# Octonion feed-forward kernel: weights loaded in 16-partition pieces from two queues, and the first ternary set ahead of x's rounding

## What is computed

```python
def ternary_dequant(W):
    scale = jnp.mean(jnp.abs(W))
    return scale * jnp.clip(jnp.round(W / scale), -1.0, 1.0)
...
gate = oct_ternary_linear(xp, w_gate)      # w_gate: 8 x 341 x 128, float32
up   = oct_ternary_linear(xp, w_up)        # w_up:   8 x 341 x 128
h    = silu(gate) * up
out  = oct_ternary_linear(hp, w_down)      # w_down: 8 x 128 x 341
```

## Time and profile before

| | |
|---|---|
| median of 3 runs | 593.52 us (593.51 to 593.63) |
| profiled execution: its own time | 593.39 us |
| profiled execution: its span | 591.4 us |
| TensorE matmul busy | 579.9 us, 98% of the span |
| VectorE, ScalarE, GpSimd busy | 510.1, 356.9, 457.3 us |
| DMA | 30.67 MB, mean 52 GB/s |

### The profile page before, as it was taken

How to read it: one execution, slowest core, us unless ns; L and a number is a source line. 1 busy time by engine, 2 the same in 40 slices (tenths; PEclk the granted TensorE clock), 3 DMA queues, 4 the chain that set the end, 5 groups by cost and what they waited for, 6 DMA issues and landing times.

```text
span 591.4 us, 16418 instructions
## 1 busy us (share of the span) xinstructions
PE 579.9 (98%) x6750; PEld 539.9 (91%) x6750; DVE 510.1 (86%) x1230; ACT 356.9 (60%) x497; POOL 457.3 (77%) x362
## 2 busy tenths in 40 slices
PE   7999999999999999999999999999999999999996
PEld 7999998899989998999989998999989998998996
DVE  4987978889997999979997999979997999958854
ACT  5788995654586456664586456664586555543540
POOL 3417569998699977998699977998699977997920
PEclk9999999999999999999999999999999999999999
DMA  9720220002210112002210212002210202002021
GB/s 208 166 73 1 72 73 2 2 2 73 108 38 1 73 54 92 3 1 73 103 42 1 74 46 99 2 2 73 97 47 2 72 3 72 2 3 72 2 73 73
DMA packets 10251, 30.67 MB, mean 52 GB/s; under 512 B 928, under 2 KB 4032, under 8 KB 10176
## 3 DMA queue, kind: packets, MB, share of 16 engines
q1 hardware_dynamic: 10176, 29.62, 15.9%
HBM read 21.23 MB, written 8.39 MB: 50 GB/s over the span
## 4 chain that ended last, share of the span: by engine, by line
POOL 50%; issue 28%; PE 7%; ACT 1%; DVE 1%; POOLq 0%; ACTq 0%
POOL hop L1382 15%; POOL hs L1376 9%; POOL hs L1372 9%; POOL hs L1377 9%; PE acc L496 5%; POOL hs L1371 5%; PE acc L391 1%; POOL r L1330 1%; ACT pk L638 0%; ACT pk L624 0%; POOL hop L1379 0%; PE acc L384 0%; ACT wd L703 0%; POOL onep L1341 0%; POOL vr L1328 0%
## 5 line engine op out<-in xcount | busy, mean ns | idle before, releaser
L496 PE MATMUL acc<-wd,hop 114*128 114x128 f16 (+1 forms) x2944 | 170.7, 219 | 0.7 <-POOL hop L1382 0.7
L496 PEld LDWEIGHTS acc<-wd,hop 114*128 114x128 f16 (+1 forms) x2944 | 167.4, 98 | 1.9 <-POOL hop L1382 0.9
L722 ACT ACTIVATE pk<-acc 114x512 f32<-114x512 f32 (+1 forms) x120 | 70.7, 590 | 83.6 <-PE acc L384 49.5
L1371 POOL TENSOR_TENSOR hs<-hx 114x512 f32<-114x512 f32 x47 | 59.8, 1273 | 55.5 <-DVE hx L1127 52.1
L1382 POOL TENSOR_TENSOR hop<-hs,hop 114x1024 f16<-114x1024 f32 x46 | 98.2, 2135 | 2.7 <-ACT hop L777 2.7
L1379 POOL TENSOR_TENSOR hop<-hx,hop 114x1024 f16<-114x1024 f32 x46 | 98.3, 2137 | 1.3 <-ACT hop L766 1.3
L384 PE MATMUL acc<-xop,wu 128*128 128x256 f16 x704 | 84.2, 273 | 1.0 <-DVE hx L1127 0.7
L1030 DVE TENSOR_TENSOR bd<-acc,pk 114x256 f32<-114x256 f32 (+1 forms) x104 | 43.5, 418 | 48.2 <-ACT pk L722 48.2
L384 PE MATMUL acc<-xop,wg 128*128 128x256 f16 x704 | 84.2, 273 | 0.1
L391 PE MATMUL acc<-xop,wu 128*128 128x256 f16 x704 | 84.1, 273 | 0.1
L391 PE MATMUL acc<-xop,wg 128*128 128x256 f16 x704 | 84.0, 273 | 0.2 <-DVE acc L1070 0.2
(11 more groups left out here) (168 smaller groups left out, 928.1 us busy)
## 6 DMA issues: line engine op xcount, KB each, us to landing
xr<-in_x SPq DMA_DIRECT2D x16, 512.0 KB, 4.2
zx<-in_x SPq DMA_DIRECT2D x16, 512.0 KB, 3.7
out_y<-zx SPq DMA_DIRECT2D x16, 512.0 KB, 2.6
hop<-in_w_down SPq DMA_DIRECT2D x1, 1364.0 KB, 19.1
hop<-in_w_gate SPq DMA_DIRECT2D x2, 576.0 KB, 9.5
hop<-in_w_up SPq DMA_DIRECT2D x1, 1152.0 KB
hop<-in_w_gate SPq DMA_DIRECT2D x1, 192.0 KB
hop<-in_w_up SPq DMA_DIRECT2D x1, 192.0 KB
```

Source lines behind the costliest of these rows:

```text
L496: last = nc.tensor.matmul(acc[:, bank[n], s // 2, at:at + P], operand(g, c, t, form, level), wd[0:WIDE[c], slot, c, :], start=which == 0 a ...
L722: nc.scalar.activation(pk[0:rows, q % 2, :, :], pair[:, :, T:2 * T], ACT.Copy, scale=XS if u[0] == "X" else 1.0).then_inc(copied, 1)
L1371: nc.gpsimd.tensor_tensor(hs[:, 4:8:2, :], h[:, 0:4:2, :], h[:, 1:4:2, :], ALU.add)
```

## The change

Gate and up are each loaded by SP's queue in seven DMAs of 16 partitions, 0 to 15 up to 96 to 111, and the last of them waits for the zeroed row. Partitions 112 and 113 of both matrices are loaded by four DMAs in ScalarE's queue, at the head of its program. All pieces of a matrix signal one semaphore, so `w_in[0]` and `w_in[1]` are waited for at 9 x 16 = 144, and `gate_rest` is gone. All 8 components of ("T",0,0) are transposed in a row after 58 idle transposes, and `total` stands ahead of ("X",0,0). Gate's absolute sums are made in two halves: VectorE components 0 to 3, ScalarE 4 to 7. ScalarE does this ahead of normalising tile 0, and `signs` ahead of `x_high`; VectorE does `ternary` ahead of `x_low`.

```diff
@@ sync
-            sp.wait_ge(row_zero, 1)
-            for lo, hi in ((96, 112), (112, 113)):
-                sp.dma_start(stage[0][lo:hi, :].rearrange("p (j e) -> p j e", j=NJ),
-                             w_gate[:, NC * lo:NC * hi, :].rearrange("j (p c) d -> p j (c d)", c=NC)).then_inc(w_in[0], 16)
...
-            for j, signal in ((0, w_in[0]), (NJ // 2, gate_rest)):
-                sp.dma_start(stage[0][0:96, :].rearrange("p (j e) -> p j e", j=NJ)[:, j:j + NJ // 2, :],
-                             w_gate[j:j + NJ // 2, 0:NC * 96, :].rearrange("j (p c) d -> p j (c d)", c=NC)).then_inc(signal, 16)
-            sp.wait_ge(row_zero, 2)
-            for lo, hi in ((0, 96), (96, 112), (112, 113)):
-                sp.dma_start(stage[1][lo:hi, :].rearrange("p (j e) -> p j e", j=NJ),
-                             w_up[:, NC * lo:NC * hi, :].rearrange("j (p c) d -> p j (c d)", c=NC)).then_inc(w_in[1], 16)
...
+            for m, w in enumerate((w_gate, w_up)):
+                for lo in range(0, 112, 16):
+                    if lo == 96:
+                        sp.wait_ge(row_zero, m + 1)
+                    sp.dma_start(stage[m][lo:lo + 16, :].rearrange("p (j e) -> p j e", j=NJ),
+                                 w[:, NC * lo:NC * (lo + 16), :].rearrange("j (p c) d -> p j (c d)", c=NC)).then_inc(w_in[m], 16)
@@ tensor
-            idle_work(62)
-            weights(("T", 0, 0), range(0, 4))
+            idle_work(58)
+            weights(("T", 0, 0))
             idle_work(4)
-            weights(("T", 0, 0), range(4, NJ))
+            total(0, ("T", 0, 0))
             x_unit(("X", 0, 0))
-            total(0, ("T", 0, 0))
             x_unit(("X", 0, 1))
@@ scalar, at the head of the program
+            for m, w in enumerate((w_gate, w_up)):
+                act.wait_ge(row_zero, m + 1)
+                act.dma_start(stage[m][112:113, :].rearrange("p (j e) -> p j e", j=NJ),
+                              w[:, NC * 112:NC * 113, :].rearrange("j (p c) d -> p j (c d)", c=NC)).then_inc(w_in[m], 16)
+                act.dma_start(stage[m][113:114, :].rearrange("p (j e) -> p j e", j=NJ)[:, :, 0:2 * DB],
+                              w[:, NC * 113:HB, :].rearrange("j (p c) d -> p j (c d)", c=2)).then_inc(w_in[m], 16)
@@ scalar, absolute(0) and its place
-                    act.wait_ge(gate_rest, 16)
-                    most = whole // 4 * 3
+                    most = whole // 2
...
+            absolute(0)
             normalise(0, 0)
-            absolute(0)
+            signs(("T", 0, 0))
             x_high(("X", 0, 0))
-            signs(("T", 0, 0))
             x_high(("X", 0, 1))
@@ vector
-            dve.wait_ge(w_in[0], 64)
+            dve.wait_ge(w_in[0], 144)
...
-            dve.wait_ge(gate_rest, 16)
-            nc.vector.tensor_reduce(asum[0:CH, 0, 1:2], stage[0][0:CH, half:half + half // 2], AX.X, ALU.add, apply_absolute_value=True).then_inc(abs_done[0], 1)
             thresholds(0, ("T", 0, 0))
+            ternary(("T", 0, 0))
             x_low(("X", 0, 0))
-            ternary(("T", 0, 0))
             x_low(("X", 0, 1))
```

More of the change, by code:

```diff
@@ L245, in octonion_ffn_attention_kernel @@
         x_in = [sem(f"x_in{t}") for t in range(NT)]; zx_in = [sem(f"zx_in{t}") for t in range(NT)]
-        w_in = [sem(f"w_in{m}") for m in range(3)]; gate_rest = sem("gate_rest"); tab_in = sem("tab_in"); out_st = sem("out_st")
+        w_in = [sem(f"w_in{m}") for m in range(3)]; tab_in = sem("tab_in"); out_st = sem("out_st")
         const_done = sem("const_done"); pchain = sem("pchain"); zeroed = sem("zeroed"); row_zero = sem("row_zero"); padded = sem("padded"); table_in = sem("table_in")
@@ L293, in _ @@
                 sp.dma_start(xr[:, t, :], x_rows[t, :, :]).then_inc(x_in[t], 16)
-            sp.wait_ge(row_zero, 1)
-            for lo, hi in ((96, 112), (112, 113)):
-                sp.dma_start(stage[0][lo:hi, :].rearrange("p (j e) -> p j e", j=NJ),
-                             w_gate[:, NC * lo:NC * hi, :].rearrange("j (p c) d -> p j (c d)", c=NC)).then_inc(w_in[0], 16)
-            sp.dma_start(stage[0][113:114, :].rearrange("p (j e) -> p j e", j=NJ)[:, :, 0:2 * DB],
-                         w_gate[:, NC * 113:HB, :].rearrange("j (p c) d -> p j (c d)", c=2)).then_inc(w_in[0], 16)
-            for j, signal in ((0, w_in[0]), (NJ // 2, gate_rest)):
-                sp.dma_start(stage[0][0:96, :].rearrange("p (j e) -> p j e", j=NJ)[:, j:j + NJ // 2, :],
-                             w_gate[j:j + NJ // 2, 0:NC * 96, :].rearrange("j (p c) d -> p j (c d)", c=NC)).then_inc(signal, 16)
-            sp.wait_ge(row_zero, 2)
-            for lo, hi in ((0, 96), (96, 112), (112, 113)):
-                sp.dma_start(stage[1][lo:hi, :].rearrange("p (j e) -> p j e", j=NJ),
-                             w_up[:, NC * lo:NC * hi, :].rearrange("j (p c) d -> p j (c d)", c=NC)).then_inc(w_in[1], 16)
-            sp.dma_start(stage[1][113:114, :].rearrange("p (j e) -> p j e", j=NJ)[:, :, 0:2 * DB],
-                         w_up[:, NC * 113:HB, :].rearrange("j (p c) d -> p j (c d)", c=2)).then_inc(w_in[1], 16)
+            for m, w in enumerate((w_gate, w_up)):
[4 more added lines that the diff above has]
+                                 w[:, NC * lo:NC * (lo + 16), :].rearrange("j (p c) d -> p j (c d)", c=NC)).then_inc(w_in[m], 16)
             sp.dma_start(down_stage, w_down.rearrange("j o h -> o j h")).then_inc(w_in[2], 16)
@@ L463, in weights @@
                     if c == 0:
-                        pe.wait_ge(w_in[m], 64 if m < 2 else 16)
-                elif m == 0 and c == 0:
-                    pe.wait_ge(gate_rest, 16)
+                        pe.wait_ge(w_in[m], 144 if m < 2 else 16)
                 for j in components:
@@ L477, in total @@
             def total(m, u):
-                pe.wait_ge(abs_done[m], 3 if m == 0 else 1)
+                pe.wait_ge(abs_done[m], 2 if m == 0 else 1)
                 nc.tensor.matmul(acc[:, bank[place[u]], 0, P - 4:P], ones[:, :], asum[:, m, :], start=True, stop=True).then_inc(total_mm, 1)
@@ L645, in absolute @@
             def absolute(m):
-                act.wait_ge(w_in[m], 64 if m < 2 else 16)
+                act.wait_ge(w_in[m], 144 if m < 2 else 16)
                 act.wait_ge(zeroed, 1)
@@ L649, in absolute @@
                 if m == 0:
-                    act.wait_ge(gate_rest, 16)
-                    most = whole // 4 * 3
+                    most = whole // 2
                     nc.scalar.activation(abs_junk[0:CH, most:whole], stage[0][0:CH, most:whole], ACT.Abs, accum_out=asum[0:CH, 0, 2:3]).then_inc(abs_done[0], 1)
                 elif m == 1:
-                    act.wait_ge(abs_done[0], 3)
+                    act.wait_ge(abs_done[0], 2)
                     nc.scalar.activation(abs_junk[0:CH, 0:whole], stage[1][0:CH, :], ACT.Abs, accum_out=asum[0:CH, 1, 0:1]).then_inc(abs_done[1], 1)
```

## The result

| | before | changed |
|---|---|---|
| median | 593.53 us (593.51 to 593.63, 4 runs) | 600.29 us (599.88 to 600.72, 4 runs) |
| ratio | | 1.0113, interval 1.0101 to 1.0126 |
| profiled execution: own time, span | 593.39, 591.4 us | 600.02, 598.2 us |
| gate's last piece acted on | 13.61 us | 17.90 us |
| first direct product | 18.20 us | 25.10 us |

The account below looks back on a forecast made before the run. The first direct product's start, set by gate's landing, was taken to bound the kernel. Later landing and order +6.2 us, clock +1.1, on the profiled 593.39 gave 600.7, as median 600.8; range 596.0 to 606.5.

Parts of the forecast that it names:

- What bounds it: TensorE is busy from the first direct product on, so each microsecond that start (18.20) moves is one of the kernel.
- The transfers: Gate's load in narrow pieces would go at 125 GB/s, landing at 17.8 us where it was acted on at 13.61.
- L: Time at which gate's load has landed and is acted on; forecast 5.0 + 1.397 MB / rate + 1.6 = 17.8 us.
- The order: Opening chain behind gate's landing: first direct product 6.6 us after it, before 4.6, as normalising now queues behind late gate.
- The clock: TensorE waiting 5.5 us for gate might fall to 1.2 GHz, slowing 28 transposes: +1.1 us, bounds 0 and 2.3.
- ScalarE's four issues: Four DMA issues at ScalarE's head, 2.4 us, first sums about 5.7 instead of 4.53; hidden by later waits, costing nothing.
- SP's queue and up: Sixteen SP issues ahead of down's instead of eleven, hidden; up lands at 29.0, within 2.2 us slack; both cost nothing.
- Overlap of neighbouring pieces: Rival: DMA engines out of step spread writes over more partitions, 180 GB/s, +2.8 us, 596.3; chance 0.20.
- Slower pieces: Rival: narrow pieces go at only 90 GB/s, gate lands at 22.1, up also late, 607.1 us; chance 0.08.
- The one-partition pieces as cause: Rival: partitions 112 and 113 cause the slow stretches, so the seven pieces go at 237 GB/s, 594.4 us; chance 0.08.
- Gate sooner, no change: Rival: runs pass at 396 GB/s, gate lands at 10.1, but idle transposes hold the product at 18.2; 593.4 us; chance 0.04.

Follow-up runs that it names:

- the spread pieces: Changed kernel with the seven 16-partition pieces each taking every seventh partition instead of neighbouring ones; 593.33 us, ratio 1.0001.
- the pieces of 32 and 64: Two versions of the changed kernel: pieces of 32 partitions (last one 16), 597.81 us; pieces of 64 and 48 partitions, 595.93 us.

## Why the prediction was right

*What bounds it.* Right, and shown: from the first product to the end of the span it is 573.1 to 573.5 us in every trace, and the transfers alone carry 5.1 of the 6.8 us.

*The transfers.* L was put at 17.8 and was 17.90, by two errors that cancel. The rate was 139 GB/s, not 125: seven narrow pieces in a row went faster than one between wide ones. The time from the last byte to the consumer was not 1.6 us: at 140 GB/s from 5 us on, x, gate and up's last two partitions, 2.47 MB, are through at 15.2, and gate is acted on at 17.90, 2.7 later. By the same sum the spread pieces are through at 10.1 and acted on at 11.71, 1.6 later, so the longer lag goes with the neighbouring partitions and not with the number of pieces. A sum of bytes by rate gives the mean DMA engine, and the landing waits for the last; the engines go on at 130 GB/s from 15 to 17 us and 143 from 17 to 19, which by the sum can only be bytes of up. That one engine is late with gate meanwhile is my reading; no view shows the engines one by one. With the right rate and the lag of before I should have said 16.7, so that L came out within 0.1 us is luck; the mechanism doesn't hang on it. The cause given, the partitions over which a transfer spreads, is borne out by the spread pieces and the pieces of 32 and 64; that the rows read, which change with the partitions, have no part in it is not shown.

*The order.* L+6.6 on full clock was put down; 6.3 was measured with the clock kept up, and 6.3 with the transfers of before. The 2 us against before's 4.6 held as a size, but not as a price of the new order: the old order with a late gate is as slow. 0.9 us of it comes back by normalising first with the order of before (5.4 behind L). For the other 0.8 no run was made; in the kernel before half of gate was there 2.5 us ahead of the rest, so that VectorE's long sum was over when the second half came, and that is the likely difference.

*The clock.* Put at +1.1 between bounds of 0 and 2.3; it fell, and cost 0.9. The pace taken for it, 182 ns, was near: 20 transposes in 4.00 us at a granted clock of 0.50 are 200 ns. Why the opening of before has that pace at a granted 1.00 stays open. The size depends on when the clock comes back: 0.5 with the last two pieces in SP's queue (product 6.9 behind L), 1.2 with the pieces of 64 (7.5), 2.0 with those of 32 (8.3), each against 6.3. Half of the upper bound was a choice between two values, and it happened to fit.

*ScalarE's four issues.* Nothing that shows, as said, though the shift was larger: the first sum started at 6.50, 2.0 late and not 1.2, since the table load, at 0.72 before, now waits behind the issues until 4.96; the statistics ended 0.7 later. *SP's queue and up.* Nothing, as said: first up product 16.5 us behind the first gate product in both kernels (41.61 and 34.70).

*The rivals.* Overlap of neighbouring pieces (596.3) fell as a case, since the rate was 139 and not 180, though 139 is above the 79 of a lone piece. It is also above the 109 that the prediction worked out as an estimate from the Trainium skill, "SBUF — State Buffer", section "Door 1: The DMA port swizzle". The argument for this rival that 0.1 MB of a narrow piece pass by 5 us doesn't follow from the rows: 1.07 MB less x's 1.049 leave 0.02. Slower pieces (607.1) fell. The one-partition pieces as cause (594.4) fell with the transfers of 112 partitions. "Gate sooner, no change" (593.4) is what the spread pieces did in the end: L = 11.71, product 18.32, no change. Its cause was another, though, the partitions and not SP's queue, and so was part of its path: gate is transposed at 12.64, behind the idle transposes, as said there, but the signs wait until 14.63 for the normalising, which had waited for the statistics.

## What to carry to other kernels

Before cutting a load into pieces, ask over which partitions the writes of one stretch of time go; 16 neighbouring partitions went at 139 GB/s, every seventh at 257, with the same pieces otherwise. In the kernel before, a single narrow transfer pulled the rate of its stretch down (125 in place of 317 GB/s) and held up what was issued ahead of it (x's second tile, 7.08 in place of 5.89). And when a transfer gets faster, look at what had been timed to its old landing: the wider transfers lowered the median by 0.7 us, and 20 idle transposes fewer by another 0.8. Idle transposes work both ways, since in the changed kernel, where they end 5 us ahead of the landing, the granted clock fell, and 0.9 us of chain went with it.

## What was not expected of the hardware

- The stretch in which mostly a lone 16-partition piece was left, behind pieces of 32, went at 79 GB/s for 2 us; seven such pieces in a row went at 139.
- 112 partitions in a transfer went at 317 GB/s from 5.5 to 7.5 us and at 271 from 8 to 16, 96 partitions at 237, with the same runs of 1536 bytes.
- A transfer can land later for what is issued behind it: x's second tile was acted on at 7.08 with the narrow piece behind it and at 5.89 without, though x's own load is the same in both. Over all versions it was 6.3 to 7.9 with 16 neighbouring partitions behind it and 5.8 to 6.1 with 112.
- The granted clock was 0.50 after a wait of 5.03 us, and also in the version with pieces of 64 partitions, from 17 to 20 us, where TensorE had waited 2.6 us for gate and then worked with shorter gaps (its x units took 3.6 us); it stayed 1.00 where the wait for gate was 1.1 to 1.6 us.
